# Destination one-hots of an edge-counting stage in another layout: chunk innermost, half-precision compare, TensorE reading at a step of five

## The reference, cut to what matters

```
for r in range(R):
    w = (edge_type == r)
    sums = segment_sum(msg * w[:, None], dst, num_segments=N)
    cnt = segment_sum(w, dst, num_segments=N)
    out = out + sums / maximum(cnt, 1.0)[:, None]      # times W_rel[r]
```

## Time and profile before

| | |
|---|---|
| three runs, median (lowest to highest) | 1009.89 us (1009.81 to 1010.46) |
| span of the profiled execution, first to last instruction | 1008.0 us |
| PE busy in the span | 925.5 us (92%) |
| DVE busy in the span | 478.0 us (47%) |
| windows 11 to 44 alternate with the first product | from 83 to 177 us |
| mean granted clock of TensorE | 0.972 of full |

### The profile page before, as it was taken

How to read it: one execution, slowest core, us unless ns; L and a number is a source line. 1 busy time by engine, 2 the same in 40 slices (tenths; PEclk the granted TensorE clock), 3 DMA queues, 4 the chain that set the end, 5 groups by cost and what they waited for, 6 DMA issues and landing times.

```text
span 1008.0 us, 14165 instructions
## 1 busy us (share of the span) xinstructions
PE 925.5 (92%) x5387; PEld 478.4 (47%) x5388; DVE 478.0 (47%) x880; ACT 336.0 (33%) x456; POOL 17.9 (2%) x46
## 2 busy tenths in 40 slices
PE   0569999899999999999999999999999999999990
PEld 0556777645444444444444444444444444444440
DVE  3589998595533333243243243233333323344881
ACT  0693445455234232132222323213223213128100
POOL 1000001000000000000000000000000000000000
PEclk9788999899999999999999999999999999999995
DMA  4401000230302220220121022022022022010010
GB/s 154 129 3 48 1 0 1 89 141 25 139 28 84 84 84 1 84 84 14 70 83 48 35 83 81 2 83 83 0 104 83 0 83 84 17 67 1 21 43 39
DMA packets 28895, 58.06 MB, mean 58 GB/s; under 512 B 1322, under 2 KB 4530, under 8 KB 28850
## 3 DMA queue, kind: packets, MB, share of 16 engines
q1 hardware_dynamic: 28849, 57.46, 16.3%
HBM read 54.90 MB, written 2.56 MB: 57 GB/s over the span
## 4 chain that ended last, share of the span: by engine, by line
PE 84%; DVE 7%; DMA 3%; issue 2%; ACT 1%; DVEq 0%; SPq 0%; POOL 0%; ACTq 0%; POOLq 0%
PE psP L712 55%; PE psA L870 17%; PE psP L674 6%; PE psA L712 4%; DMA x<-in_x 3%; PE psP L788 1%; PE psA L663 1%; DVE stats L1186 1%; DVE wsplit L1013 1%; DVE p_mem L1035 1%; DVE wsplit L1106 1%; ACT wsplit L402 0%; DVE p_mem L1337 0%; DVE x L1208 0%; DVE p_mem L1339 0%
## 5 line engine op out<-in xcount | busy, mean ns | idle before, releaser
L712 PE MATMUL psP<-wsplit,xT 128*128 128x512 f16 x2400 | 521.6, 379 | 0.8 <-DVE u_mem L1251 0.8
L712 PEld LDWEIGHTS psP<-wsplit,xT 128*128 128x128 f16 x2400 | 234.8, 98 | 282.9 <-DVE u_mem L1251 1.3
L1233 DVE SCALAR_TENSOR_TENSOR p_mem<-psP,p_mem 128x512 f16<-128x512 f32 x80 | 55.3, 691 | 283.9 <-ACT p_mem L598 282.4
L598 ACT ACTIVATE p_mem<-psP 128x512 f16<-128x512 f32 x80 | 47.8, 597 | 403.1 <-PE psP L712 403.1
L870 PE MATMUL psA<-p_mem,c_mem 128*128 128x512 f16 x800 | 175.4, 379 | 1.4 <-DVE u_mem L1251 1.4
L870 PEld LDWEIGHTS psA<-p_mem,c_mem 128*128 (+1 forms) x800 | 78.2, 98 | 96.0 <-DVE u_mem L1251 1.9
L1251 DVE SCALAR_TENSOR_TENSOR u_mem<-psA,coef,u_mem 128x512 f32<-128x512 f32 x80 | 60.0, 751 | 101.6 <-PE psA L870 101.6
L1013 DVE SCALAR_TENSOR_TENSOR wsplit<-stage,sc,wsplit 128x4096 f16<-128x4096 f32 (+1 forms) x22 | 97.4, 4429 | 9.3 <-ACT wsplit L444 9.3
L674 PE MATMUL psP<-p_mem 125*128 125x140 f16 x1125 | 78.9, 233 | 24.0 <-DVE p_mem L1035 15.9
L674 PEld LDWEIGHTS psP<-p_mem 125*128 125x128 f16 x1125 | 76.0, 102 | 28.5 <-issue 15.6
L444 ACT ACTIVATE wsplit<-stage,sc 128x4096 f16<-128x4096 f32 (+1 forms) x22 | 80.6, 3663 | 23.2 <-DVE sc L936 18.6
(11 more groups left out here) (151 smaller groups left out, 364.5 us busy)
## 6 DMA issues: line engine op xcount, KB each, us to landing
stage<-in_L_gnn_weight SPq DMA_DIRECT2D x16, 2048.0 KB, 7.8
stage<-in_L_gnn_w_gate SPq DMA_DIRECT2D x4, 2048.0 KB, 7.7
stage<-in_L_gnn_W_rel SPq DMA_DIRECT2D x4, 572.0 KB, 11.7
x<-in_x SPq DMA_DIRECT2D x1, 2048.0 KB
xT<-in_L_gnn_root SPq DMA_DIRECT2D x1, 2048.0 KB, 7.9
stage<-in_L_gnn_root SPq DMA_DIRECT2D x1, 2048.0 KB, 8.0
out<-x SPq DMA_DIRECT2D x4, 512.0 KB
stage<-in_L_gnn_W_root SPq DMA_DIRECT2D x2, 572.0 KB, 13.3
```

The costliest lines, as they stand in the source:

```text
L598: nc.scalar.activation(p_part[slot][0][:, t, :], psP[:, t, :], ACT.Copy, scale=PROD_GAIN).then_inc(p_hi, 1)
L712: last = nc.tensor.matmul(out, lhs[:, a, c, bass.ts(t, P)], w[:, c, cols], start=first, stop=(c == chunks - 1 and a == 1))
L1233: ins = stt(p_part[slot][1][:, t, :], src, PROD_GAIN, p_part[slot][0][:, t, :], ALU.mult, ALU.subtract)
```

## The change

The destination one-hots of a buffer are laid out with the chunk as the innermost index, [column][chunk] where it was [chunk][column]. The column keys stand in a new constant `iota_rep`, each repeated five times, which two more `iota` instructions on GpSimd fill. For each window one small `tensor_scalar` subtracts the window's base from the ten keys of its five chunks and writes them in f16. VectorE waits for this result through a new semaphore. Then two `tensor_tensor` compares in f16, without a scalar operand, write the one-hots of all five chunks. TensorE's moving operand is then `oh_win[:, b, :, k]`, 140 elements of 2 bytes at a step of five elements, 10 bytes. `consts_ready` is waited for at 14. The source one-hots, the matmuls' number and shape, and the copies stay.

```diff
+        iota_rep = sb("iota_rep", [P, WCOLS, MEET], F16)
+        win_key = sb("win_key", [EC, 2, 2, MEET], F16)
...
-        oh_win = win_mem[:, 0:2 * MEET * WCOLS].rearrange("p (b k n) -> p b k n", b=2, k=MEET)
+        oh_win = win_mem[:, 0:2 * MEET * WCOLS].rearrange("p (b n k) -> p b n k", b=2, k=MEET)
...
+            nc.gpsimd.iota(iota_rep[:, 0:WIN * R1, :].rearrange("p (w r) k -> p w r k", r=R1),
+                           pattern=[[16, WIN], [1, R1], [0, MEET]], base=0, **loose).then_inc(consts_ready, 1)
+            nc.gpsimd.iota(iota_rep[:, WIN * R1:WCOLS, :].rearrange("p (w r) k -> p w r k", r=R0),
+                           pattern=[[16, WIN], [1, R0], [0, MEET]], base=0, **loose).then_inc(consts_ready, 1)
...
-            act.wait_ge(consts_ready, 12)
+            act.wait_ge(consts_ready, 14)
...
-                    last = count_chunk(b, oh_src[:, b, k, :], oh_win[:, b, k, :], k == 0)
+                    last = count_chunk(b, oh_src[:, b, k, :], oh_win[:, b, :, k], k == 0)
...
-            dve.wait_ge(consts_ready, 12)
+            dve.wait_ge(consts_ready, 14)
...
-                for a, w, cols in ((1, win8, slice(0, WIN * R1)), (2, win2, slice(WIN * R1, WCOLS))):
-                    n = w.shape[1]
-                    stt(oh_win[:, b, :, cols], w.unsqueeze(1).broadcast_to([EC, MEET, n]), wb,
-                        keyT[:, bass.ds(chunk, MEET), a:a + 1].broadcast_to([EC, MEET, n]), ALU.add, ALU.is_equal)
+                ts(win_key[:, b, :, :].rearrange("p a k -> p k a"), keyT[:, bass.ds(chunk, MEET), 1:3], wb, None,
+                   ALU.subtract).then_inc(win_key_ready, 1)
+                dve.wait_ge(win_key_ready, j + 1)
+                for a, cols in ((0, slice(0, WIN * R1)), (1, slice(WIN * R1, WCOLS))):
+                    n = cols.stop - cols.start
+                    tt(oh_win[:, b, cols, :], iota_rep[0:EC, cols, :],
+                       win_key[:, b, a, :].unsqueeze(1).broadcast_to([EC, n, MEET]), ALU.is_equal)
```

More of the change, by code:

```diff
@@ L187, in build @@
         table_ready = sem("table_ready")
+        win_key_ready = sem("win_key_ready")
         onehot_free = sem("onehot_free")
```

## The result

The changed kernel takes 1104.8 us (median of four, 1102.7 to 1105.8) against 1010.2 us before: the ratio is 1.093, 95% interval 1.092 to 1.095. It is slower, as forecast, but by 95 us where 16 were forecast, and outside the range. The span of the profiled execution is 1104.0 us against 1008.0.

The account below looks back on a forecast made before the run. PE was taken as the bound, busy 925.5 of 1008.0 us, with only TensorE on the chain from 83 to 177 us. 1008.0 + 15.6 + 1.4 - 1.2 = 1023.8 us, 1025.7 with 1.9 around it; range 1007.5 to 1070 us.

Parts of the forecast that it names:

- TensorE's read at a step: Moving read of all 1125 counting matmuls, 850 on the chain without cover: 15.6 us more for 34 windows.
- I take the factor: TensorE's stepped moving read costs 1.30 times its time, as VectorE's copy L968: 0.46 us a window; chance 0.32.
- the far end: TensorE's stepped read priced as time per byte of step: 1.13 ns a column, 2.42 us more a window, 1092 us and more.
- half rate or worse: Rival: the step halves TensorE's rate or worse, 1.58 us more on each of 34 windows, 1064.7 us; chance 0.27.
- The three counts before 83 us: TensorE's counting of three windows on the chain before 83 us, 0.46 us more each: 1.4 us.
- move as a block: The product, the copies and all that follow the counting matmuls shift later together.
- VectorE's gain: VectorE's f16 compares at two elements a step shrink a window by 0.20 us, 1.2 us in all.
- six windows: VectorE's one-hots of six windows on the chain between 36 and 83 us, each 0.20 us shorter: 1.2 us.
- GpSimd: Two more iota over 560 and 140 elements delay consts_ready and VectorE's first two windows by 0.87 us, hidden.
- The cover: VectorE's 7.27 us wait for the norms after its first two windows was to hide the delay from the new constants.

Follow-up runs that it names:

- the pairs: Kernel before, with each key written twice side by side and f16 compares reading keys and columns in twos, TensorE's read untouched: 1009.2 us, ratio 0.9990.
- both kernels in which TensorE reads adjacent elements: The changed kernel with TensorE reading 140 adjacent elements of the same buffer, 1009.55 us; the kernel before with VectorE's compares reading in pairs, 1009.2 us.
- one pattern of short runs: Kernel before with a constant of zeros as moving operand, one chunk reading seven adjacent elements of every eight: 0.35 us for five matmuls, 0.31 expected.
- the run with pairs across a block: Kernel before with a constant of zeros as moving operand, read in pairs across or inside 16-byte blocks, sevens and fours; counts left out: 1082.3 us.

## Why the prediction was wrong

**The term that was mis-sized: TensorE's read at a step.** The step of the argument that failed is "I take the factor", 0.46 us a window. It measured 2.41. The row was the right one: the stepped copy L968, 1.35 ns an element at 12 bytes. Of its two readings I took the factor of 1.30 over VectorE's own time for an element. The other reading, a time of 1.13 ns a column, was given as the far end, and it is what was measured, 157.4 ns a matmul where it said 158. TensorE pays a time for each block, and at the step of five that time does not follow its clock (157 ns a matmul at a clock of 1.00, 159 at 0.50). A share of the engine's own time was therefore the wrong thing to carry over. TensorE wants a column every 0.42 ns, VectorE an element every 1.04. If the same block time holds on both, what adds 30% there adds 158% here. That both times come so close for L968 is suggestive: 12 bytes are three quarters of a block, and 1.35 / 0.75 = 1.80 ns. It may also be luck, since L968 is a write of f32 with its source in PSUM, and the 1.04 ns beside it come from another instruction. No run tested VectorE's side.

The case that came true is the rival "half rate or worse", with a chance of 0.27, at its far end; its reason, that a limit in time bites harder on the engine that asks more often, is what the runs show. Its first price, half the rate (3.11 us a window, 1064.7 us), was also too low. The range left out the far end, which the working itself had put at 1092 and more, so it was cut against its own bound. Taken through the prediction's own sum, the far end gives 1009.9 + 82.4 + 3 * 2.42 - 1.2 = 1098.4 us, against 1105.8 for the profiled execution; 5.4 of the missing 7.4 us are the clock.

The two rules of the Trainium skill can now be set against rows. "Advanced Engine Details and Errata", section "Memory Cachelines", says that SBUF has 16-byte lines: the runs agree, with the price flat from 16 bytes on and doubled by an offset across a line. It also asks for at least two hits on a line for the full rate: here two were not enough. At a step of four, two columns to a line, five matmuls took 0.63 us instead of 0.31. A line's 1.79 ns is the time of 4.3 columns at full clock. "SBUF — State Buffer", in the section "Door 1: The DMA port swizzle", has a step of up to eight bf16 as free: the step of eight took 1.25 us.

**What follows from it.** The three counts before 83 us were to add 1.4 us, and the place where the alternation starts came 8.4 us later, since the chain there turned to TensorE, with seven windows on it instead of three. The product's pieces were to move as a block; they grew by 5.4 us by the clock, which no term had.

**VectorE's gain.** Forecast 0.20 us a window, from instructions of 450, 232 and some 231 ns. They took 509, 241 and 246, and windows follow by 2.34 us (28.48 to 30.82) instead of 2.48 (24.92 to 27.40), 0.14 us. With the pairs the two compares take 451 and 225 ns, as forecast; what makes the rows of five slower was not tried. The two kernels differ in the constant that they read and in the order of their writes, too. The Trainium skill's rule on f16 two-source instructions ("VectorE: DVE Perf Modes", "The perf-mode tier table") agrees with the 451 ns. The gain was to reach the end through six windows, 1.2 us. In both kernels in which TensorE reads adjacent elements the second piece of the product starts 0.8 us earlier, but only three windows of VectorE are on their chains, and with the pairs the chain from 67 us on goes through ScalarE and TensorE. So the "six windows" did not hold: once VectorE is faster, others end last. That the size came near is in part luck.

**GpSimd.** Forecast 0.87 us for the two constants. The timeline of the changed kernel:

```profile
11.06 2.28 POOL L372 IOTA iota_rep<- 128x560 f16 x1
13.30 0.69 POOL L374 IOTA iota_rep<- 128x140 f16 x1
13.95 0.09 POOL L376 MEMSET ones<- 128x1 f16 x1
...
37.51 0.19 DVE L1089 RECIPROCAL rstd<-std 128x5 f32<-128x5 f32 x1 [4.26 <-ACT std L412]
```

It is 2.9 us (11.06 to 13.95), more than three times as much, and VectorE's first window starts 3.6 us later, at 28.48 instead of 24.92 us. The cover was where I said: VectorE's wait for the norms shrank from 7.27 us to 4.26. The norms came 0.3 us later, and so did the end of the load of x on the chain.

The direction was right, and so was the place: 81.9 of the 96.0 us fall on the 850 matmuls with no cover. The kind of cost was not.

## What to carry to other kernels

Before a layout makes a TensorE moving operand stepped, count the blocks of 16 bytes that it enters: the price is close to the larger of 0.42 ns a column and 1.79 ns a block (one pattern of short runs took a tenth more). A step on the stationary operand was free here, up to eight elements beside matmuls of 61 ns. The pairs gave VectorE a gain at least as large with no step in any of TensorE's reads. And when a stepped access of one engine has to price another's, work out both the ratio and the time, and let the range reach over both: here the time was right.

## What the runs showed of the hardware that was not expected

- TensorE's moving read of 2-byte elements pays 1.79 ns for each new aligned block of 16 bytes and nothing for the distance: steps of 3, 4, 5, 6, 8 and 16 elements give 0.48, 0.63, 0.79, 0.93, 1.25 and 1.27 us for five matmuls of 140 columns. At a step of five it does not follow TensorE's clock: 157 ns a matmul at 1.00, 159 at 0.50.
- A step of up to 8 elements on the stationary operand of 128 columns cost nothing beside matmuls of 61 ns.
- Slow reads can lower the granted clock though TensorE counts as busy throughout: to 0.83 in the alternation of the changed kernel, which cost 5.4 us on matmuls that were not changed, and to 0.59 to 0.74 at steps of 6 to 16. Not all do: in the run with pairs across a block a window took 3.50 us instead of 3.93, and the clock stayed at 1.00:

```profile
130.00:150.00 20.00, 20.00 (x133) 13.85 (x132) 12.08 (x34) 4.30 (x17) 0.00 (x0) 1.00 0.00 0
```

- An `iota` on GpSimd with rows of five took 2.28 us for 560 elements, where one row of 640 took 0.66.
